# Spectral mixing in 32x32 blocks with shorter seams between the layers of a Fourier tower

## The chip, the cores and the metric

The kernel runs on one core of one Trainium2 chip. The metric is the device time of one execution in microseconds (us). Engines are named as in the profile: PE is TensorE (matmuls), PEld its weight loads, DVE is VectorE, ACT is ScalarE, POOL is GpSimd, SP is SyncE, which issues most DMAs.

## The reference, cut to what matters

A tower of four Fourier layers on 64 images of 64x64 pixels and 32 channels, a two-layer head to one value per pixel, then an attention and an expert stage (the second half, which the change leaves as it is):

```python
x = coords @ fc0_w + fc0_b                             # lift 3 -> 32 channels
for sw, cw, cb in layers:                              # 4 layers
    x_ft = rfft2(x, norm='ortho')
    out = einsum('bixy,ioxy->boxy', x_ft[:, :, :20, :20], sw)   # the mix
    x1 = irfft2(out padded to 64x33, norm='ortho')
    x2 = einsum('bchw,oc->bohw', x, cw) + cb
    x = gelu(x1 + x2)
x = gelu(x @ fc1_w + fc1_b) @ fc2_w + fc2_b
```

Only 20x20 frequencies of each image are kept. The mix multiplies, at each of these 400 frequencies, a 32x32 matrix of channels by the 32 channels of 64 images (real and imaginary part: 128 columns).

## The kernel before

All data is fp32, and each fp32 matmul is two weight loads and two matmul records in the trace (a high and a low part). The Fourier transforms are matmuls with constant tables, and between them DVE turns 32x32 blocks (STREAM_TRANSPOSE) so that the next axis comes to lie on the partitions.

The tower works on pairs of images (32 pairs, index t or j). Per layer it has two parts.

The mix (`mix`, line 478): it needs all images, so it stands between the layers. `modes` holds the frequencies: its partitions are four blocks of 32, block b = 2*kwh + khh, where kwh is the half of the row frequency kw (kw = 10*kwh + k) and khh the half of kh. For each k of 10 and each m of 10, two matmuls of 64x64 (kwh 0 and 1) with 128 columns run. Their weights are `mode_w`, two 32x32 matrices on the diagonal of a 64x64 block whose other half is zeros that the host wrote; they come by DMA in a ring of five k. The sums of one k fill four PSUM banks; two sets of four banks take turns. ACT copies the first half of a k (line 767), DVE the second (line 711) back into `modes` as 128x640, and the matmuls of k wait for the copies of k-2.

The pair loop: for each pair DVE turns the modes (`turn_modes`, line 679), PE does the inverse transform over h (`inverse_h`, line 491, banks 4 to 7), DVE turns the result (`turn_inverse`, line 689), PE adds the 1x1 convolution (`conv`, line 511: 16 matmuls of 32x32 on all 16 blocks of the array, banks 0 to 3) and the inverse transform over w (`inverse_w`, line 524, four parts, banks 0 to 3), ACT applies GELU (line 774) and stores the result. In the same loop, two and three pairs behind, the next layer's forward transform starts: DVE turns the activations (`turn_act`, line 654), PE does `dft_w` (line 429, banks 4 to 7), DVE `turn_w` (line 665), PE `dft_h` (line 441, banks 0 and 1), DVE `turn_h` (line 671), which writes `modes`. The loop of a layer has three extra rounds (j = 32 to 34) for the last forward transforms. `keep_busy` (line 517) are matmuls on constants whose result nobody reads; 8 stand behind the first `inverse_h` of a layer, 6 + 4 + 6 in the extra rounds, 10 ahead of the next mix.

The start: SP loads the identity (for the second half), the two forward tables, the first two quarters of the input, then it waits for the zeroed tiles (`zeroed`) and loads 14 small constants for the lift (`lift_consts`), then the later quarters and the rest. PE transforms four quarters of the input; 8 `lift` matmul groups (line 458, four 32x32 blocks each, ACT copies, line 759) follow each of them one quarter behind. DVE builds `lift_w` from the constants between `turn_w(0)` and `turn_w(1)` (line 698). Eight matmuls (line 545) that build the first layer's convolution weights stand ahead of the last lifts, and DVE copies them (line 705).

Every engine works through its list in the order written; waits are on semaphores.

Of the kernel before, what the change touches and what calls it, by code (L numbers as in the profile page):

```python
# [23 lines left out]
RING_W = 5  # L24
PAD_N = 96
MIXES = MODES // 2
GROUP = 16
# [19 lines left out]
def dft_constants():  # L47
# [39 lines left out]
    places = np.concatenate([np.arange(MODES // 2), 16 + np.arange(MODES // 2)])  # L87
# [120 lines left out]
def tower(nc, banks, front, h_dram, wqkv, k_rope, k_decay, x, x_turned, fc0, fc0_t, sw, cwt, cb, fc1_w, fc1_b, fc2_w, fc2_b,  # L208
# [4 lines left out]
    with ExitStack() as ctx:  # L213
# [24 lines left out]
        mode_w = sb("mode_w", [128, RING_W, MODES // 2, 2 * CH])  # L238
# [20 lines left out]
        fwd_in = sem("fwd_in")  # L259
# [6 lines left out]
        mode_w_in = [sem(f"mode_w_in{s}") for s in range(RING_W)]  # L266
# [13 lines left out]
        mixed = [sem(f"mixed{half}") for half in range(2)]  # L280
# [37 lines left out]
        def after_mix(l, k):  # L318
            return l * MIXES + k + 1
# [17 lines left out]
        def mix_sums(rows_b, k):  # L337

            return banks[rows_b, k % 2 * 4:k % 2 * 4 + 4, :].rearrange("p b n -> p (b n)")
# [11 lines left out]
        def _(sp):  # L351

            def load_mode_w(l, k):

                n = l * MIXES + k
                if n >= RING_W:
                    sp.wait_ge(mixed[1], n - RING_W + 1)
                sp.dma_start(flat(mode_w[:, n % RING_W]), sw[l, k]).then_inc(mode_w_in[n % RING_W], 16)
# [27 lines left out]
            for k in range(RING_W):  # L386
                load_mode_w(0, k)
            for q in range(2):
                sp.dma_start(flat(xin[:, q]), x[q]).then_inc(xin_in[q], 16)
            for l in range(LAYERS):  # L390
                for k in range(RING_W, MIXES):
                    load_mode_w(l, k)
                if l + 1 < LAYERS:
                    for k in range(RING_W):
                        load_mode_w(l + 1, k)
# [26 lines left out]
        def _(pe):  # L422

            def dft_w(n):

                for wh in range(2):
                    for i in range(2):
# [7 lines left out]
            def dft_h(n, parity):  # L435

                pe.wait_ge(w_turned, after_w_turned(n, 1))
                for ph in range(2):
                    for i in range(2):
                        for kwh in range(2):  # L440
                            mm = nc.tensor.matmul(banks[kwh * 64:(kwh + 1) * 64, i, 0:320],  # L441
# [7 lines left out]
            def lift(q, e):  # L449
# [4 lines left out]
                else:  # L454
                    pe.wait_ge(lift_w_set, 1)
                for b in range(4):
# [5 lines left out]
            def mix(l):  # L462
# [5 lines left out]
                for k in range(MIXES):  # L468
                    n = l * MIXES + k
                    pe.wait_ge(mode_w_in[n % RING_W], 16 * (n // RING_W + 1))  # L470
                    if k >= 2:
                        pe.wait_ge(mix_out["act"], after_mix(l, k - 2))
                        pe.wait_ge(mix_out["dve"], after_mix(l, k - 2))
                    for m in range(MODES // 2):
                        at = m // 5 * 2 * 512 + m % 5 * 128
                        for kwh in range(2):
                            rows_b = slice(kwh * 64, (kwh + 1) * 64)
                            mm = nc.tensor.matmul(mix_sums(rows_b, k)[:, at:at + 128],  # L478
                                                  mode_w[rows_b, n % RING_W, m, :],
                                                  modes[rows_b, :, k, 2 * m:2 * m + 2], start=True, stop=True)  # L480
                        if m % 5 == 4:
                            mm.then_inc(mixed[m // 5], 1)

            def inverse_h(l, t):

                pe.wait_ge(modes_turned, after_inverse(l, t))
                for i in range(2):
# [9 lines left out]
            def conv(l, t):  # L497

                if t > 0:
                    pe.wait_ge(inv_turned, after_inv_turned(l, t, 1))  # L500
                    pe.wait_ge(act_set, after_out(l, t - 1, 3))
                if l == 0:
# [11 lines left out]
            def keep_busy(n):  # L514

                for _ in range(n):
                    nc.tensor.matmul(banks[:, 3, 0:128], inv_w[:, 0, :], inv_w[:, 0, :], start=True, stop=True)
# [12 lines left out]
            pe.wait_ge(fwd_in, 32)  # L530
            pe.wait_ge(xturned_in[0], 16)
            dft_w(0)
            for q in range(QUARTERS):
# [7 lines left out]
                if q > 0:  # L541
                    for e in range(LIFT_E):
                        lift(q - 1, e)
            for e in range(LIFT_E):
                mm = nc.tensor.matmul(banks[:, 4, e * CH:(e + 1) * CH],
                                      fc0_cols[:, e].rearrange("c p e k -> c (p e k)"), conv_w[0:CH, 0, :],
                                      start=True, stop=True)
            mm.then_inc(first_w_filled, 1)
# [4 lines left out]
            pe.wait_ge(first_w_set, 1)  # L553

            for l in range(LAYERS):
# [3 lines left out]
                keep_busy(8)  # L559
                for j in range(PAIRS + (0 if last else 3)):  # L560
                    if j > PAIRS:
                        if j == PAIRS + 1:
                            pe.wait_ge(act_set, after_out(l, PAIRS - 1, 3))
                        keep_busy(6)
                    if j == 0:
                        conv(l, 0)
# [7 lines left out]
                    if j < PAIRS:  # L574
                        if j >= 4 and not last:
                            pe.wait_ge(modes_set, forward(l + 1, j - 4) + 1)
                        if j > 0:
                            conv(l, j)
                        for p in range(2):
                            inverse_w(l, j, p)  # L580
                    if 0 <= j - 2 < PAIRS and not last:
# [3 lines left out]
                        elif j >= PAIRS:  # L585
                            pe.wait_ge(w_turned, after_w_turned(forward(l + 1, j - 3), 1))
                        dft_w(forward(l + 1, j - 2))
                    if j < PAIRS:
                        for p in range(2, 4):
                            inverse_w(l, j, p)  # L590
                    if 0 <= j - 3 < PAIRS and not last:
                        if j < PAIRS:
                            pe.wait_ge(act_set, after_out(l, j, 1))
                        else:
# [1082 lines left out]
```

## Time and profile before

| what | value |
|---|---|
| runs | 1740.77, 1744.27, 1749.69 us (median 1744.27) |
| the profiled execution | 1742.08 us, its span 1740.3 us |
| PE / PEld / DVE / ACT / POOL busy | 94% / 55% / 69% / 34% / 8% |
| start up to the first mix | 0 to 53.9 us |
| the four mixes | 53.9 to 76.1, 390.8 to 412.9, 727.7 to 749.8, 1064.5 to 1086.7 us |
| between two mixes | 314.7 us each, three times |
| after the last mix | 653.6 us |

The span is the time from the first to the last instruction. The profiled execution lies 2.2 us under the median of the runs. A line of the trace's timeline has the start, the duration, engine, line and operation, output and inputs, the number of instructions merged, and in brackets the idle time before it and who ended it. A busy PE is one with a matmul in flight, and not one at its peak: a mix has PE busy all the time and uses two of four 64x64 blocks of the array.

### The profile page before, as it was taken

The page shows a single profiled execution, that of the slowest core. Times are in us where ns is not written, and L with a number is a line of the kernel's source. Part 1 is how long each engine was busy: PE and PEld are TensorE (multiplying, and loading weights), DVE is VectorE, ACT ScalarE, POOL GpSimd, SP SyncE. Part 2 cuts the span into 40 slices and gives each one's busy share as a digit, 9 for nine tenths or more (in the row PEclk, how much of TensorE's full clock was granted, in tenths as well). Part 3 has the DMA queues.
Part 4 walks back from the last instruction along what each step waited for, and adds up shares of the span by engine and source line. Part 5 has one row for each costly group of instructions (what it writes and reads, how often), then busy time and mean ns, then how long its engine had stood idle before and what let it go on. Part 6 is the DMA issues. An engine that isn't in the chain of part 4 may idle for free. (4 is left out here: it accounts for less than half of the span.)

```text
span 1740.3 us, 44221 instructions
## 1 busy us (share of the span) xinstructions
PE 1634.5 (94%) x20058; PEld 959.0 (55%) x20058; DVE 1201.5 (69%) x1406; ACT 585.3 (34%) x783; POOL 140.1 (8%) x64
## 2 busy tenths in 40 slices
PE   7999999999999999999999999999988888989996
PEld 2765555558555555775555557777741117833332
DVE  3389898875898898578898984555510007956777
ACT  2332232213232222232222322444468885510000
POOL 1000000000000000000000000000000000057664
PEclk9999999999999999999999999999999999999998
DMA  5233233244656556456556563699996642075551
GB/s 197 77 134 135 122 123 123 104 189 127 263 204 235 218 221 236 159 173 237 219 218 236 205 240 112 234 347 352 363 343 239 228 166 89 13 182 149 145 142 37
DMA packets 67706, 327.86 MB, mean 188 GB/s; under 512 B 19200, under 2 KB 21184, under 8 KB 33600
## 3 DMA queue, kind: packets, MB, share of 16 engines
q1 hardware_dynamic: 44736, 189.63, 33.3%
q10 hardware_dynamic: 22784, 135.41, 18.9%
q8 instruction: 159, 2.61, 0.6%
q14 instruction: 27, 0.22, 0.0%
HBM read 187.64 MB, written 137.36 MB: 187 GB/s over the span
## 5 line engine op out<-in xcount | busy, mean ns | idle before, releaser
L774 ACT ACTIVATE act_c<-slots,conv_b 128x512 f32<-128x512 f32 x512 | 352.3, 688 | 741.4 <-PE slots L524 741.4
L524 PEld LDWEIGHTS slots<-inv_w,inv_out 128*128 128x128 f32 x4096 | 499.1, 196 | 179.0 <-issue 179.0
L524 PE MATMUL slots<-inv_w,inv_out 128*128 128x128 f32 x4096 | 540.7, 287 | 0.0
L689 DVE STREAM_TRANSPOSE inv_out<-slots 128x1024 f32<-128x1024 f32 x256 | 304.5, 1228 | 101.0 <-PE slots L491 101.0
L665 DVE STREAM_TRANSPOSE turned_h<-slots 128x1024 f32<-128x1024 f32 x200 | 237.7, 1227 | 34.1 <-PE slots L429 33.8
L654 DVE STREAM_TRANSPOSE turned_w<-act_c 128x1024 f32<-128x1024 f32 x192 | 225.1, 1214 | 0.0
L429 PE MATMUL slots<-turned_w,fwd_w 32*64 32x512 f32 x3200 | 200.8, 609 | 13.0 <-DMA fwd_h<-in_k_fwd_h_dram 7.1
L1598 POOL TENSOR_TENSOR modes<-at_turned,modes 128x1024 f32<-128x1024 f32 x14 | 34.6, 2477 | 1545.7 <-DMA at_turned<-level_scratch 1530.6
L785 ACT ACTIVATE inv_out<-slots,b 128x1024 f32<-128x1024 f32 x128 | 135.7, 1111 | 20.8 <-PE slots L613 20.8
L671 DVE STREAM_TRANSPOSE modes<-slots 128x640 f32<-128x640 f32 x96 | 81.4, 848 | 88.2 <-PE slots L441 88.2
L441 PE MATMUL slots<-turned_h,fwd_h 64*64 64x320 f32 x1600 | 137.1, 455 | 0.0
L511 PE MATMUL slots<-act_c,conv_w 32*32 32x512 f32 x3072 | 110.7, 599 | 20.3 <-DVE modes L671 14.9
L491 PE MATMUL slots<-turned_k,inv_h 32*64 32x320 f32 x2048 | 101.9, 453 | 8.6 <-DVE turned_k L679 7.2
L429 PEld LDWEIGHTS slots<-turned_w,fwd_w 32*64 32x64 f32 x3200 | 60.2, 132 | 79.8 <-issue 61.8
L679 DVE STREAM_TRANSPOSE turned_k<-modes 128x640 f32<-128x640 f32 x128 | 102.9, 806 | 0.1
L1133 PE MATMUL slots<-modes,ex_lattice_w 128*64 128x512 f32 x344 | 89.3, 622 | 11.4 <-DVE modes L1340 5.8
L613 PE MATMUL slots<-act_c,w 32*64 32x512 f32 x1024 | 71.5, 612 | 21.7 <-ACT inv_out L785 20.9
L478 PE MATMUL slots<-modes,mode_w 64*64 64x128 f32 x1600 | 88.6, 267 | 0.8 <-ACT modes L759 0.8
L478 PEld LDWEIGHTS slots<-modes,mode_w 64*64 64x64 f32 x1600 | 87.7, 130 | 1.9 <-issue 1.5
L1340 DVE TENSOR_TENSOR modes<-slots,modes 128x512 f32<-128x512 f32 x102 | 65.2, 684 | 32.5 <-PE slots L1116 31.7
L746 DVE TENSOR_SCALAR modes<-slots,b 128x512 f32<-128x512 f32 x4 | 3.0, 751 | 113.9 <-PE slots L624 113.9
L711 DVE COPY modes<-slots 128x640 f32<-128x640 f32 x40 | 33.0, 824 | 69.7 <-PE slots L478 69.7
(145 smaller groups left out, 1057.4 us busy)
## 6 DMA issues: line engine op xcount, KB each, us to landing
act_scratch<-act_c ACTq DMA_DIRECT2D x128, 1024.0 KB, 4.9
act_c<-act_scratch SPq DMA_DIRECT2D x128, 1024.0 KB, 5.2
mode_w<-in_sw_dram SPq DMA_DIRECT2D x40, 320.0 KB, 3.0
at_turned<-level_scratch SPq DMA_DIRECT2D x36, 256.0 KB, 4.2
at_ret_t<-level_scratch SPq DMA_DIRECT2D x34, 256.0 KB, 4.1
turned_w<-in_x_turned_dram SPq DMA_DIRECT2D x4, 1024.0 KB, 5.7
xin<-in_x_dram SPq DMA_DIRECT2D x4, 1024.0 KB, 7.5
at_straight<-level_scratch SPq DMA_DIRECT2D x16, 256.0 KB, 4.1
```

The source lines that it names most:

```text
L429: mm = nc.tensor.matmul(banks[i * 64:(i + 1) * 64, 4 + p, :], fwd_w[p * 32:(p + 1) * 32, wh, :], turned_w[p * 32:(p + 1) * 32, n % 2, wh, ...
L441: mm = nc.tensor.matmul(banks[kwh * 64:(kwh + 1) * 64, i, 0:320], fwd_h[i * 64:(i + 1) * 64, parity, ph, :], turned_h[i * 64:(i + 1) * 64, ...
L478: mm = nc.tensor.matmul(mix_sums(rows_b, k)[:, at:at + 128], mode_w[rows_b, n % RING_W, m, :], modes[rows_b, :, k, 2 * m:2 * m + 2], start ...
L491: mm = nc.tensor.matmul(banks[half * 64:(half + 1) * 64, 4 + 2 * i + kwh, 0:320], inv_h[b * 32:(b + 1) * 32, l % 2, :], turned_k[b * 32:(b ...
L511: nc.tensor.matmul(banks[q * 32:(q + 1) * 32, p, :], w, src, start=True, stop=False, skip_group_check=True)
L524: mm = nc.tensor.matmul(banks[:, p, at:at + 128], inv_out[:, t % 2, i, p, :, :, r].rearrange("p b o -> p (b o)"), inv_w[:, i, :], start=Fa ...
L654: last = nc.vector.transpose(dst, src)
L665: nc.vector.transpose(dst, src).then_inc(w_turned, 1)
L679: nc.vector.transpose(dst, src).then_inc(modes_turned, 1)
L689: nc.vector.transpose(dst, src).then_inc(inv_turned, 1)
L774: nc.scalar.activation(act_c[:, t % RING, :, p, :], banks[:, p, :].rearrange("p (i m) -> p i m", i=2), ACT.Gelu, bias=conv_b[:, l:l + 1]). ...
L785: nc.scalar.activation(unit[:, n % 2, a:a + 2, :], banks[:, at:at + 2, :], ACT.Gelu, bias=b1[:, 0:1]).then_inc(unit_set, 1)
```

## The change

- The mix weights are stored as 32x32 matrices without the zeros (half the bytes); all ten k of a layer have their place in `mode_w`, loaded two k at a time.
- For an even k a block's result stays in its own partitions (b to b), for an odd k it goes to the other half's (b to b^2). An even and an odd k are mixed together (`side` 0 and 1), so 8 different 32x32 blocks of the array are named one after the other, then again for the next kh. The inverse table over w (`places`) undoes the exchange.
- A step u covers five kh of two k: 40 matmuls. After each, ACT copies side 0 and DVE side 1 (128x640 each), and step u waits for the copies of u-2.
- Behind the last step, both copy four images first (`few_set`), DVE turns the modes of pair 0, and then they copy the other 60 images. `keep_busy(8)` goes; `conv(0)` and the first part of `inverse_w(0)` come ahead of `inverse_h(1)`.
- The three extra rounds of a layer become a written-out tail: two of its `dft_h` use banks 2 and 3, so that they needn't wait for the `turn_h` of banks 0 and 1; `turn_act(31)` and `turn_w(30)` come ahead of `turn_h(28)`; 26 `keep_busy` matmuls become 6.
- `dft_h` waits for the two halves of `turn_w` one by one.
- Start: the first half of quarter 0 is loaded first, in a DMA of its own; the identity later; the lift constants are issued by ACT; 7 and 6 matmuls on zeros stand around the first `dft_w`; the eight matmuls for the first convolution weights come behind `dft_h(0)`, and ACT copies them.

```diff
-    places = np.concatenate([np.arange(MODES // 2), 16 + np.arange(MODES // 2)])
+    kw = np.arange(MODES)
+    place, kwh = kw % MIXES, kw // MIXES
+    places = 16 * (kwh ^ place % 2) + place
...
-            sp.dma_start(flat(fwd_w[:]), k_fwd_w).then_inc(fwd_in, 16)
-            sp.dma_start(flat(turned_w[:, 0]), x_turned[0]).then_inc(xturned_in[0], 16)
-            sp.dma_start(flat(fwd_h[:]), k_fwd_h).then_inc(fwd_in, 16)
+            sp.dma_start(flat(turned_w[:, 0, 0]), x_turned[0, :, 0:1024]).then_inc(first_half_in, 16)
+            sp.dma_start(flat(fwd_w[:]), k_fwd_w).then_inc(fwd_w_in, 16)
+            sp.dma_start(flat(turned_w[:, 0, 1]), x_turned[0, :, 1024:2048]).then_inc(xturned_in[0], 16)
             sp.dma_start(flat(turned_w[:, 1]), x_turned[1]).then_inc(xturned_in[1], 16)
-            sp.wait_ge(zeroed, 1)
-            for dst, src in lift_consts:
-                sp.dma_start(dst, src).then_inc(lift_in, 16)
+            sp.dma_start(flat(fwd_h[:]), k_fwd_h).then_inc(fwd_h_in, 16)
...
-                for k in range(MIXES):
-                    n = l * MIXES + k
-                    pe.wait_ge(mode_w_in[n % RING_W], 16 * (n // RING_W + 1))
-                    if k >= 2:
-                        pe.wait_ge(mix_out["act"], after_mix(l, k - 2))
-                        pe.wait_ge(mix_out["dve"], after_mix(l, k - 2))
-                    for m in range(MODES // 2):
-                        at = m // 5 * 2 * 512 + m % 5 * 128
-                        for kwh in range(2):
-                            rows_b = slice(kwh * 64, (kwh + 1) * 64)
-                            mm = nc.tensor.matmul(mix_sums(rows_b, k)[:, at:at + 128],
-                                                  mode_w[rows_b, n % RING_W, m, :],
-                                                  modes[rows_b, :, k, 2 * m:2 * m + 2], start=True, stop=True)
-                        if m % 5 == 4:
-                            mm.then_inc(mixed[m // 5], 1)
+                for u in range(MIX_STEPS):
+                    if u % 2 == 0:
+                        pe.wait_ge(mode_w_in[u // 2], 16 * (l + 1))
+                    if u >= 2:
+                        pe.wait_ge(mix_out["act"], after_mix(l, u - 2))
+                        pe.wait_ge(mix_out["dve"], after_mix(l, u - 2))
+                    for m in range(5):
+                        for side in range(2):
+                            for b in range(4):
+                                to = b ^ 2 * side
+                                rows_b, rows_to = slice(b * 32, (b + 1) * 32), slice(to * 32, (to + 1) * 32)
+                                k, kh = u // 2 * 2 + side, u % 2 * 5 + m
+                                mm = nc.tensor.matmul(mix_sums(rows_to, side, u % 2)[:, m * 128:(m + 1) * 128],
+                                                      mode_w[rows_b, u // 2, side, kh, :],
+                                                      modes[rows_b, :, k, 2 * kh:2 * kh + 2], start=True, stop=True)
+                    mm.then_inc(mixed, 1)
...
                 inverse_h(l, 0)
-                keep_busy(8)
+                conv(l, 0)
+                pe.wait_ge(inv_turned, after_inv_turned(l, 0, 1))
+                inverse_w(l, 0, 0)
+                inverse_h(l, 1)
+                for p in range(1, 4):
+                    inverse_w(l, 0, p)
...
                 if not last:
-                    keep_busy(10)
+                    parity = (l + 1) % 2
+                    ends = [forward(l + 1, PAIRS - 3 + i) for i in range(3)]
+                    pe.wait_ge(act_turned, after_turn(l + 1, PAIRS - 2))
+                    pe.wait_ge(w_turned, after_w_turned(ends[0], 1))
+                    dft_w(ends[1])
+                    pe.wait_ge(act_set, after_out(l, PAIRS - 1, 3))
+                    keep_busy(4, 3)
+                    dft_h(ends[0], parity, at=2)
+                    pe.wait_ge(act_turned, after_turn(l + 1, PAIRS - 1))
+                    pe.wait_ge(w_turned, after_w_turned(ends[1], 1))
+                    dft_w(ends[2])
+                    pe.wait_ge(modes_set, ends[0])
+                    dft_h(ends[1], parity)
+                    pe.wait_ge(modes_set, ends[0] + 1)
+                    dft_h(ends[2], parity, at=2)
+                    keep_busy(2, 4)
...
+                dve.wait_ge(mixed, after_mix(l, MIX_STEPS - 1))
+                nc.vector.tensor_copy(*mix_part(MIX_STEPS - 1, 1, slice(0, 4))).then_inc(few_set["dve"], 1)
+                dve.wait_ge(mix_out["dve"], after_mix(l, MIX_STEPS - 2))
+                dve.wait_ge(few_set["dve"], l + 1)
+                dve.wait_ge(few_set["act"], l + 1)
                 turn_modes(l, 0)
+                nc.vector.tensor_copy(*mix_part(MIX_STEPS - 1, 1, slice(4, IMAGES))).then_inc(mix_out["dve"], 1)
+                turn_inverse(l, 0)
                 turn_modes(l, 1)
-                turn_inverse(l, 0)
...
+                if not last:
+                    turn_act(l + 1, PAIRS - 1)
+                    turn_w(forward(l + 1, PAIRS - 2))
+                    for t in range(PAIRS - 4, PAIRS):
+                        if t == PAIRS - 2:
+                            turn_w(forward(l + 1, PAIRS - 1))
+                        turn_h(forward(l + 1, t), modes[:, 2 * t:2 * t + 2],
+                               at=2 if t in (PAIRS - 3, PAIRS - 1) else 0)
```

## Rows read from the trace of the kernel before

**Rows 1.** The page's head: the span of the profiled execution.

```profile
span 1740.3 us, 44221 instructions
```

**Rows 2.** Busy time by stretch: first mix, all up to the second.

```profile
53.93:76.10 22.17, 22.14 (x400) 21.94 (x400) 7.42 (x9) 7.29 (x11) 0.00 (x0) 1.00 0.45 134
76.10:390.80 314.70, 303.92 (x4166) 184.21 (x4165) 273.55 (x257) 89.08 (x129) 0.00 (x0) 1.00 0.34 130
```

**Rows 3.** Timeline of the second mix: PE, ACT's first copy, DVE's last copy.

```profile
390.80 22.15 PE L478 MATMUL slots<-modes,mode_w 64*64 64x128 f32 x400
...
392.16 0.69 ACT L767 COPY modes<-slots 128x640 f32<-128x640 f32 x1 [17.04 <-PE slots L478]
...
413.00 0.82 DVE L711 COPY modes<-slots 128x640 f32<-128x640 f32 x1 [1.37 <-PE slots L478]
```

**Rows 4.** DVE's copy line by itself: min, median and max in ns.

```profile
L711 DVE COPY modes<-slots x40: 823/825/825, 56.5 to 1086.7; 128x640 f32<-128x640 f32 x40
```

**Rows 5.** Timeline: matmuls on 32x32 blocks, a convolution and eight lifts.

```profile
22.95 6.00 PE L458 MATMUL slots<-act_c,lift_w 32*32 32x400 f32 x64
...
87.30 0.27 PEld L511 LDWEIGHTS slots<-xin,first_w 32*32 32x32 f32 x32 [0.63 <-issue]
87.33 1.15 PE L511 MATMUL slots<-xin,first_w 32*32 32x512 f32 x32
...
88.42 4.04 PE L524 MATMUL slots<-inv_w,inv_out 128*128 128x128 f32 x32
```

**Rows 6.** Timeline behind the second mix, PE and DVE.

```profile
413.85 1.57 DVE L679 STREAM_TRANSPOSE turned_k<-modes 128x640 f32<-128x640 f32 x2
414.75 0.80 PE L491 MATMUL slots<-turned_k,inv_h 32*64 32x320 f32 x16 [1.80 <-DVE turned_k L679]
...
415.66 2.38 DVE L689 STREAM_TRANSPOSE inv_out<-slots 128x1024 f32<-128x1024 f32 x2 [0.23 <-PE slots L491]
...
418.54 0.85 PE L491 MATMUL slots<-turned_k,inv_h 32*64 32x320 f32 x16
...
419.31 4.04 PE L524 MATMUL slots<-inv_w,inv_out 128*128 128x128 f32 x32
...
423.28 0.79 PE L491 MATMUL slots<-turned_k,inv_h 32*64 32x320 f32 x16
```

**Rows 7.** Timeline of a layer's last rounds, PE and DVE.

```profile
372.42 2.38 DVE L665 STREAM_TRANSPOSE turned_h<-slots 128x1024 f32<-128x1024 f32 x2 [3.04 <-PE slots L429]
...
374.32 1.36 PE L441 MATMUL slots<-turned_h,fwd_h 64*64 64x320 f32 x16
...
375.61 1.97 PE L429 MATMUL slots<-turned_w,fwd_w 32*64 32x512 f32 x32
...
376.52 2.33 DVE L654 STREAM_TRANSPOSE turned_w<-act_c 128x1024 f32<-128x1024 f32 x2
...
388.37 2.50 PE L517 MATMUL slots<-inv_w 128*128 128x128 f32 x20
388.51 0.85 DVE L671 STREAM_TRANSPOSE modes<-slots 128x640 f32<-128x640 f32 x1 [1.98 <-PE slots L441]
```

**Rows 8.** Timeline of the start: SP, PE and DVE.

```profile
6.49 4.23 SPq L380 DMA_DIRECT2D fc_cols<-in_fc_t_dram  x8
...
7.07 3.72 PE L429 MATMUL slots<-turned_w,fwd_w 32*64 32x512 f32 x32 [7.07 <-DMA fwd_h<-in_k_fwd_h_dram]
...
14.70 0.43 DVE L698 TENSOR_TENSOR lift_w<-fc_rows,lift_mask 128x256 f32<-128x256 f32 x1 [1.42 <-DMA fc_cols<-in_fc_t_dram]
...
19.76 1.98 PE L429 MATMUL slots<-turned_w,fwd_w 32*64 32x512 f32 x32 [0.73 <-DVE turned_h L665]
...
45.25 1.97 PE L545 MATMUL slots<-conv_w,fc_cols 32*128 32x32 f32 x16
...
47.25 0.42 DVE L705 COPY first_w<-slots 128x256 f32<-128x256 f32 x1 [6.96 <-PE slots L545]
```

**Rows 9.** A stretch without matmuls in the second half; the clock stands behind POOL.

```profile
1536.00:1540.00 4.00, 0.00 (x0) 0.00 (x0) 0.00 (x0) 0.00 (x0) 2.21 (x1) 0.67 0.99 237
```

More of the change, by code:

```diff
@@ L23 @@
 RING = 4
-RING_W = 5
 PAD_N = 96
 MIXES = MODES // 2
+MIX_STEPS = MIXES
 GROUP = 16
@@ L279, in tower @@
         lift_out = sem("lift_out")
-        mixed = [sem(f"mixed{half}") for half in range(2)]
+        mixed = sem("mixed")
         mix_out = {"dve": sem("mix_out_dve"), "act": sem("mix_out_act")}
@@ L334, in after_store, with mix_sums @@
             return 16 * (l * (PAIRS // RING) + t // RING + 1)
-        def mix_sums(rows_b, k):
-            return banks[rows_b, k % 2 * 4:k % 2 * 4 + 4, :].rearrange("p b n -> p (b n)")
+        def mix_sums(rows, side, half):
+            at = 4 - 4 * side + 2 * half
+            return banks[rows, at:at + 2, :].rearrange("p b n -> p (b n)")
         def head_bank(n, a):
@@ L385, in _ @@
                 sp.dma_start(dst, src).then_inc(rest_in, 16)
-            for k in range(RING_W):
-                load_mode_w(0, k)
+            sp.dma_start(ident[:, :], k_ident).then_inc(ident_in, 16)
+            for pair in range(MIXES // 2):
+                load_mode_w(0, pair)
             for q in range(2):
@@ L422, in _, with warm_up @@
         def _(pe):
+            def warm_up(n):
+                for _ in range(n):
+                    nc.tensor.matmul(banks[:, 3, 384:512], w2_at[:, 0:128], w2_at[:, 0:128], start=True, stop=True)
             def dft_w(n):
                 for wh in range(2):
+                    if n == 0 and wh == 1:
+                        pe.wait_ge(xturned_in[0], 16)
                     for i in range(2):
@@ L512, in conv, with keep_busy @@
                                          skip_group_check=True)
-            def keep_busy(n):
+            def keep_busy(n, b):
                 for _ in range(n):
-                    nc.tensor.matmul(banks[:, 3, 0:128], inv_w[:, 0, :], inv_w[:, 0, :], start=True, stop=True)
+                    nc.tensor.matmul(banks[:, b, 384:512], inv_w[:, 0, :], inv_w[:, 0, :], start=True, stop=True)
             def inverse_w(l, t, p):
@@ L540, in _ @@
                 dft_h(q, 0)
-                if q > 0:
+                if q == 0:
+                    pe.wait_ge(lift_in, LIFT)
+                    for e in range(LIFT_E):
+                        mm = nc.tensor.matmul(banks[:, 3, e * CH:(e + 1) * CH],
+                                              fc0_cols[:, e].rearrange("c p e k -> c (p e k)"), conv_w[0:CH, 0, :],
+                                              start=True, stop=True)
+                    mm.then_inc(first_w_filled, 1)
+                else:
                     for e in range(LIFT_E):
                         lift(q - 1, e)
[L544 to L548, printed above, removed]
             pe.wait_ge(modes_set, QUARTERS)
@@ L558, in _ @@
                 inverse_h(l, 0)
-                keep_busy(8)
[L560 to L566, printed above, removed]
+                conv(l, 0)
[4 more added lines that the diff above has]
+                    inverse_w(l, 0, p)
+                for j in range(1, PAIRS):
                     if j + 1 < PAIRS:
@@ L573, in _ @@
                         inverse_h(l, j + 1)
[L574 to L581, printed above, removed]
+                    if j >= 4 and not last:
+                        pe.wait_ge(modes_set, forward(l + 1, j - 4) + 1)
+                    conv(l, j)
+                    for p in range(2):
+                        inverse_w(l, j, p)
+                    if j >= 2 and not last:
                         pe.wait_ge(act_turned, after_turn(l + 1, j - 2))
@@ L584, in _ @@
                             pe.wait_ge(inv_turned, after_inv_turned(l, j + 1, 1))
-                        elif j >= PAIRS:
-                            pe.wait_ge(w_turned, after_w_turned(forward(l + 1, j - 3), 1))
                         dft_w(forward(l + 1, j - 2))
[L588 to L594, printed above, removed]
-                            pe.wait_ge(modes_set, forward(l + 1, j - 4) + 1)
-                        if j == PAIRS + 1:
-                            keep_busy(4)
+                    for p in range(2, 4):
+                        inverse_w(l, j, p)
+                    if j >= 3 and not last:
+                        pe.wait_ge(act_set, after_out(l, j, 1))
                         dft_h(forward(l + 1, j - 3), (l + 1) % 2)
                 if not last:
-                    keep_busy(10)
+                    parity = (l + 1) % 2
[14 more added lines that the diff above has]
+                    keep_busy(2, 4)
             pe.wait_ge(act_set, after_out(LAYERS - 1, PAIRS - 1, 3))
@@ L756, in _ @@
         def _(act):
+            act.wait_ge(zeroed, 1)
+            for dst, src in lift_consts:
+                act.dma_start(dst, src).then_inc(lift_in, 16)
+            act.wait_ge(first_w_filled, 1)
+            nc.scalar.copy(flat(first_w[:]), banks[:, 3, 0:LIFT_E * CH]).then_inc(first_w_set, 1)
             for n in range(PAIRS):
@@ L1635 @@
     sw = sw.transpose(0, 5, 4, 1, 6, 3, 2)
-    paired = _np.zeros(sw.shape[:6] + (2, CH), _np.float32)
-    for khh in range(2):
-        paired[:, :, khh, :, :, :, khh] = sw[:, :, khh]
     x = _np.concatenate([f["x"], _np.ones((IMAGES, HH, WW, 1), _np.float32)], axis=3)
```

100 lines of the change are left out of this document (55 added, 45 removed).

## The prediction

> **What bounds the kernel now.** I read the busy time by stretch first. Each of the four mixes is a stretch of 22.2 us in which PE runs the whole time while DVE and ACT are busy a third of it [rows 2]; the stretch between two mixes takes 314.7 us, 303.9 of them with matmuls in flight [rows 2]. PE sets the pace in both. The change leaves a pair's work alone, so I take the pair loop at nothing and look at three places: the mixes, the seams on either side of them, and the start. I read each in the timeline.
>
> **The mix.** 400 records take 22.15 us [rows 3], so 55.4 ns each. A record's 128 columns would pass at 2.4 GHz in 53 ns; a fp32 record takes two passes (107 ns), and two blocks run side by side. So the mix is bound by columns, with 110.8 ns per round of two blocks. After the change there are 800 records in rounds of eight blocks: 10 rounds per step (five kh, high and low part), 10 steps, 100 rounds. The trace of before has no round of eight blocks with 128 columns. The nearest is the convolution: 32 records of 32x32 on 16 blocks, with 512 columns, take 1.09 us up to the next line's start (87.33 to 88.42), and their 32 loads together cover 0.27 us, so each follows the last by some 5 ns [rows 5]. In a round of 110.8 ns eight starts fit at that spacing, so I take 110.8 ns for the new round too, and 1.11 us for a step.
>
> Then the copies. Before, ACT's first copy starts 1.36 us after the first of ten rounds [rows 3]; eight blocks instead of two stagger the end by some 0.05, so 1.41. DVE's copy takes 0.82 [rows 4], and I allow 0.05 back to PE: 2.28 us for the two steps that share the banks, 1.14 per step against PE's 1.11. Copies and matmuls nearly balance. The last copy can start after 4 x 2.28 + 1.11 + 1.41 = 11.64 us, where before it started after 22.20 (390.80 to 413.00) [rows 3]. That is 10.56 less. Weights: half the bytes, all resident a layer ahead; their wait is hidden as before, by the 300 us pair loop.
>
> At this place the Trainium skill speaks against the change. In "TensorE: Matmul & The Clock Gate", section "Wait — 56ns, not 53.3ns?", it says that matmuls never start closer than about 25 ns, however few columns they have. By that 800 records take 20 us, and a mix would give back 2 us instead of 10.6. The loads and blocks in [rows 5] start closer than that, so here the trace disagrees, though in bursts only.
>
> **Behind the mix.** Before: copy 0.82, turn of pair 0, and `inverse_h(0)` starts 1.75 us after the copy's start (413.00 to 414.75) [rows 3, 6]. Now a copy of four images (40 elements) stands in place of 640. From 0.82 for 640 [rows 4] and 0.42 for 256 [rows 8] it comes to 0.20, so 0.62 less. ACT's second copy (0.69 [rows 3]) ends under the turn. So far 11.18 per mix.
>
> From `inverse_h(0)` to `inverse_h(2)`, before, 8.53 us [rows 6], with 8 `keep_busy` among them. Now, counted from `inverse_h(0)`: DVE copies 60 images up to 0.75 (hidden, since the turn waits for the 0.91 of `inverse_h` anyway, as 414.75 to 415.66); `turn_inverse(0)` to 3.29, `turn_modes(1)` to 4.10; PE's convolution lies under it; `inverse_w(0,0)` 3.35 to 4.50 (8 records at 0.118 and a drain of 0.2); `inverse_h(1)`; DVE turns its result from 5.41 to 7.79, then the modes of pair 2 to 8.6: `inverse_h(2)` at 8.67. So DVE takes the place of `keep_busy` and 0.14 is lost. Per layer 11.04, four times: 44.2 us.
>
> **Ahead of the mix** (three times). Before, `dft_h(28)` starts at 374.32 and the mix at 390.80, 16.48 later; the last `turn_h` ends at 389.36, and 20 records of `keep_busy` hold PE another 1.4 us [rows 3, 7]. Now: DVE ends `turn_w(29)` at 374.80, does `turn_act(31)` to 377.5 (its input, ACT's last GELU, is in at 375.15), waits for `dft_w(30)` (375.61, done at 377.7), `turn_w(30)` to 380.05, `turn_h(28)`, `turn_h(29)` to 381.7. PE meanwhile: 8 records of `keep_busy`, `dft_h(29)` into the other banks, idle to 380.1, `dft_w(31)` to 382.1, `dft_h(30)`. DVE `turn_w(31)` 382.2 to 384.55, `turn_h(30)` to 385.4; `dft_h(31)`'s second half ends at 385.4, `turn_h(31)` at 386.3. Mix at 386.35: 4.45 less, 13.35 in all. Durations: 2.38, 2.33, 0.85, 1.90, 1.29 [rows 7]. The new tail is one chain of turns and transforms; what is late next is DVE.
>
> **The start.** Before, `dft_w(0)` takes 3.72 us at 7.07 and `dft_w(2)` 1.98 at 19.76 [rows 8]: the same work at half the speed, so PE's clock was at its lower level (1.2 GHz) at first. The matmuls on zeros and the earlier first half (half of the bytes, and the identity no longer ahead) bring `dft_w(0)` forward by some 3 us. But DVE must build `lift_w` before `turn_w(1)`, from 14 small DMAs. Now ACT issues them from about 2.5 (after the zeroing); at SP's pace (8 in 4.23 us [rows 8], 14 in 7.65) the last is out at 10.15, and it landed 3.98 after its issue (10.72 to 14.70 [rows 8]): 14.1, or 13.1 with a shorter landing. I take 13.7. Then `turn_w(1)` ends at 16.5, and `dft_w(2)` starts at 16.65: 3.1 less (2.0 to 4.7). The 1.9 us of matmuls for the first weights [rows 8] go into PE's wait for that turn. Together 5.0.
>
> **Sum.** 44.2 + 13.35 + 5.0 = 62.5; 1742.08 - 62.5 = 1679.6 on the profiled execution, whose span is 1740.3 [rows 1]. It ran 2.2 us below the median. I say 1680.
>
> **Rivals.**
> 1. Slower: dispatch, not columns, paces a long run. 55.4 ns per record [rows 3] would then be the price of a record of any size, and 800 take 44.3 us: 22.15 more per mix, 88.6 in all, less the other gains (62.5 - 42.2 = 20.3): 1810. It decides from 27.2 us per mix, that is 34 ns per record. Against it: the convolution's 32 records average 34 with four times the columns, and 64 lifts in 6.0 us wait for ACT half of the time [rows 5]. But both are short bursts behind a wait, and a mix is 1600 PE instructions without pause. 0.05.
> 2. A floor on starts of up to 34 ns, the convolution's average [rows 5]: 27.2 us per mix, 1742, no change. 0.05. With the page's 25 ns it would be 20 us per mix and 1713.
> 3. Blocks that share 32 rows take turns, since even and odd k stream different data through the same rows: a mix stays at 22.15, only the rest is gained: 1722. The convolution streams four through the same rows in 2 x 512 columns' time [rows 5]; against that its data lies dense and the mix's in 8-byte pieces. 0.07.
> 4. Copies set the pace: they balance with PE within 3%, so a quarter more on the step (1.14 to 1.43) costs 2.9 per mix: 1691. 0.08.
> 5. The clock falls in a seam, since `keep_busy` goes. The trace shows the granted clock at a mean of 0.67 in a stretch without any matmul, 1536 to 1540 [rows 9], and PE had 1.80 us idle ahead of `inverse_h(0)` at full clock [rows 6]. The new gaps are 1.2 to 1.5 us, two close together. Half speed for 7 us costs 3.5 per seam, 14 in all: 1694. 0.10.
> 6. More than forecast, from a start that is not held by the constants or a seam without drains: 1673 to 1668. 0.07.
>
> **How the numbers follow.** The forecast has 0.58. The range goes from 1668 to 1706: it holds the forecast and cases 4 to 6 and leaves out 1 to 3 (0.17). A measurement of this kernel can tell about 0.5% (9 us) from no change. Slower is case 1; same is most of case 2; all else is faster: 0.91, 0.04, 0.05.
>
> **What would show it.** Line 478's successor: 800 records of 32x32 in about 11.5 us per mix, DVE's copies following each other at 1.14 us; at 22 it is case 3, at 44 case 1, and copies without gaps mean case 4. A granted clock of 1.00 between the mixes rules out case 5. From one mix's start to the next, 336.9 us before, I expect 321.4. `dft_w` of the third quarter near 16.7 us. The prediction is wrong if a mix takes over 13 us, or if the pair loop, which I took at nothing, moves.

## The result and the profile after

The change makes the kernel faster, by less than half of what was forecast: 1725.38 us in the median of four runs (1721.60 to 1725.98) against 1744.53 before (four runs), a ratio of 0.987 with an interval of 0.984 to 0.991. The prediction said 1680, with 1668 to 1706 as its range. The profiled execution took 1721.60 us, its span 1719.6. Medians below are of all executions of a kernel; ratios and intervals leave out the few that were disturbed, such as two of the twelve of e7_old_start, whose median without them is 1739.9.

The spans differ by 20.7 us. The table goes stage by stage; each number, in us, is the difference of two starts in the timelines of the two kernels.

| stage | before | after | forecast |
|---|---|---|---|
| start up to the first mix | 53.9 | 50.8 | 48.9 |
| mix's first matmul to `inverse_h(0)`, four mixes | 23.95 each | 21.5, 24.2, 22.1, 21.3 | 12.8 each |
| `inverse_h(0)` to `inverse_h(2)` | 8.53 each | 8.7, 9.3, 9.3, 9.2 | 8.67 each |
| `dft_h(28)` to the mix, three times | 16.48 each | 12.17, 12.17, 12.18 | 12.03 each |

So 3.1 came from the start, 6.8 from the mixes, 12.9 from the seams ahead of them, and the seams behind them cost 2.4: 20.4 in all. The pair loop, taken at nothing, took its old time. What is missing against the forecast is almost all in the mixes: 44.7 us were expected from that row, 6.8 came.

The first mix after, PE alone, in the timeline (start, duration, engine, line, operation, number of records, idle time before and its cause); before, a mix was one line of 22.15 us without a gap (the second mix, [rows 3]):

```profile
50.84 3.81 PE L491 MATMUL slots<-modes,mode_w 32*32 32x128 f32 x239 [0.66 <-issue]
...
55.53 2.18 PE L491 MATMUL slots<-modes,mode_w 32*32 32x128 f32 x127 [0.88 <-issue]
...
59.02 2.26 PE L491 MATMUL slots<-modes,mode_w 32*32 32x128 f32 x127 [1.30 <-issue]
...
62.44 2.04 PE L491 MATMUL slots<-modes,mode_w 32*32 32x128 f32 x128 [1.16 <-issue]
...
66.00 2.29 PE L491 MATMUL slots<-modes,mode_w 32*32 32x128 f32 x127 [1.52 <-issue]
...
69.97 1.06 PE L491 MATMUL slots<-modes,mode_w 32*32 32x128 f32 x52 [1.68 <-issue]
```

Two things are to be seen. Inside a burst (records without a pause between them) the blocks of the array work nearly as forecast: 239 records in 3.81 us are 16 ns each, eight array blocks side by side. And every 127 or 128 records PE stands still for 0.9 to 1.7 us, for no engine and no DMA ("issue"). 128 records and their 128 weight loads are 256 instructions. The page of the kernel after shows the same number in its list of DMA queues:

```profile
q8 instruction: 170, 2.79, 0.7%
```

170 packets carry 2.79 MB, 16.4 KB each, while PE has 43,000 matmul and load instructions in all: 253 per packet, some 64 bytes for an instruction. The Trainium skill, "Vector Engine (DVE) Microarchitecture Reference", section "2.1 Why there are multiple struct shapes", gives 64 bytes as the width of every instruction; the trace agrees for PE. PE's program comes from memory by DMA, a block of 256 instructions at a time, and in the mix the blocks come more slowly than eight array blocks use them up. By stretch, the first and the last mix after. The columns are the stretch, its length, the busy time (number) of PE, PEld, DVE, ACT and POOL, the granted clock, the busy share of the DMA engines and GB/s:

```profile
50.84:71.10 20.26, 13.65 (x800) 11.40 (x800) 7.44 (x10) 6.26 (x10) 0.00 (x0) 1.00 0.23 69
...
1045.72:1065.70 19.98, 13.60 (x800) 11.49 (x800) 7.42 (x9) 6.25 (x9) 0.00 (x0) 1.00 0.02 4
```

PE is busy 13.6 us of 20; its four hundred matmuls are twice as many as before. The last mix has nearly no DMA traffic beside it (4 GB/s) and takes as long as the first with 69, so it isn't the other transfers that set the pace of the instructions. That they cost them nothing is not shown: in the second mix, with 112 GB/s, the bursts start 3.8 to 3.9 us apart, in the last 3.4 to 3.7.

### The profile page after: what moved, and what is told of

Read it like the earlier page. It is cut to its first block and busy times, and to the rows that moved or that the text cites. A ratio compares the mean times of both kernels' runs of the same rounds, so it can differ in the third digit from the quotient of the medians.

```text
span 1719.6 us, 47103 instructions
## 1 busy us (share of the span) xinstructions
PE 1587.7 (92%) x21500; PEld 900.3 (52%) x21500; DVE 1201.3 (70%) x1409; ACT 585.9 (34%) x788; POOL 140.4 (8%) x64
## 3 DMA queue, kind: packets, MB, share of 16 engines
q8 instruction: 170, 2.79, 0.7%
## 5 line engine op out<-in xcount | busy, mean ns | idle before, releaser
L439 PEld LDWEIGHTS slots<-turned_w,fwd_w 32*64 32x64 f32 x3200 | 59.6, 131 | 69.4 <-issue 54.4
L638 PE MATMUL slots<-act_c,w 32*64 32x512 f32 x1024 | 71.5, 612 | 22.1 <-ACT inv_out L831 20.5
L491 PE MATMUL slots<-modes,mode_w 32*32 32x128 f32 x3200 | 54.5, 268 | 31.1 <-issue 30.1
L451 PEld LDWEIGHTS slots<-turned_h,fwd_h 64*64 64x64 f32 x1600 | 51.2, 131 | 46.2 <-issue 5.4
```

The costliest lines, as they stand in the source:

```text
L451: mm = nc.tensor.matmul(banks[kwh * 64:(kwh + 1) * 64, at + i, 0:320], fwd_h[i * 64:(i + 1) * 64, parity, ph, :], turned_h[i * 64:(i + 1) ...
```

## The experiments

Theory A: the supply of instructions, one block of 256 in no less than about 3.5 us. Its rivals: B, array blocks that share rows collide; a price per start; C, the copies set the pace.

**e1_sides64.** Four 64x64 blocks in place of eight of 32x32. The exchange between the halves stays, the zeros come back, and 800 instructions do for 1600. The weights come in ten portions of 320 KB per layer, five of them resident.

```diff
-                            for b in range(4):
-                                to = b ^ 2 * side
-                                rows_b, rows_to = slice(b * 32, (b + 1) * 32), slice(to * 32, (to + 1) * 32)
+                            for b in range(2):
+                                to = b ^ side
+                                rows_b, rows_to = slice(b * 64, (b + 1) * 64), slice(to * 64, (to + 1) * 64)
```

> The changed kernel with the mix weights again as 64x64 blocks with zeros (as before), but with even and odd k mixed together and exchanged between the halves as in the change: four 64x64 blocks at once, 200 matmuls (800 PE instructions) per mix in place of 400 (1600). Theory A, instruction supply: in the changed kernel's mixes PE works in bursts of 127 or 128 records with pauses of 1.3 to 1.9 us, and a 16 KB instruction packet arrives every 3.4 to 3.9 us; 800 instructions need no more than three of them, so the mix takes what the array needs, 100 rounds of 0.11 us: 11.3 to 13 us, without pauses, and the time falls from 1725 by about 35 to 1690 us. Theory B, the streams: different data streamed through the same rows collide; this kernel does that too, so its mix stays at 20 to 22 us and the time at 1722 to 1730. Theory C, the copies set the pace: steps stay as long as they are, 1725.

Measured: 1690.46 us, 0.967 of the kernel before (0.964 to 0.970). The first two mixes, PE:

```profile
53.12 12.34 PE L494 MATMUL slots<-modes,mode_w 64*64 64x128 f32 x400 [0.66 <-issue]
...
375.39 7.78 PE L494 MATMUL slots<-modes,mode_w 64*64 64x128 f32 x256 [0.33 <-DVE modes L700]
384.46 4.37 PE L494 MATMUL slots<-modes,mode_w 64*64 64x128 f32 x144 [1.29 <-issue]
```

A mix takes 12.2 to 13.4 us from its first record to the end of its last. The first and the fourth have no pause, the second has a single one, behind record 256, and the third one of 0.54 us: a little more than A had allowed (11.3 to 13 us, no pauses). The time fell as A said. B and C are out for this kernel, whose streams share rows and whose copies are the same. 64 of these matmuls are one block of instructions and take 3.9 us (half of the 7.78), so the array runs at the edge of the supply. In a second set of executions the same kernel took 1694.03 (e6_sides64_again, 0.970, 0.967 to 0.973).

> The same kernel as e1_sides64, for comparison on one chip: 0.966 to 0.967 of the kernel before; first mix between 50.8 and 53.1 us, by the landing of the constants.

**e3_diagonal64.** The same without the exchange (`to = b`, and the old `places`).

> As the first kernel of this set (64x64 blocks, 800 PE instructions per mix), but without the exchange between the halves: only the two blocks on the diagonal work, with the changed kernel's seams and start. Theory A: bound by columns like the kernel before, 200 rounds of 0.11 us, 22.2 us per mix without pauses; about 1 us more per layer than the changed kernel, 1726 to 1732 us. Against e1 it gives the worth of the exchange alone (about 40 us by A, none by B).

```profile
53.50 22.15 PE L494 MATMUL slots<-modes,mode_w 64*64 64x128 f32 x400 [0.66 <-issue]
```

Measured: 1729.63 us, 0.990 of before (0.984 to 0.995); every mix 22.15 us without a pause. The exchange, which lets all four 64x64 blocks work, is worth 39 us on the same chip (1729.63 to 1690.46). The run also gives the worth of all that isn't the mix's matmuls: 20.7 us in the medians (1750.28 to 1729.63), but with an interval of 8 to 28. Its profile shows 14.7 up to the start of the fourth mix. What follows `inverse_h(0)` of the last layer, most of it the second half, which none of the changes touches, takes from 651.8 (before) to 659.0 us (here) in the profiles without a probe.

**e2_half_columns.** The changed kernel with 64 columns per matmul, so that it leaves half of the mix out; eight matmuls at the start write zeros into all banks. One execution.

```diff
-                                mm = nc.tensor.matmul(mix_sums(rows_to, side, u % 2)[:, m * 128:(m + 1) * 128],
+                                mm = nc.tensor.matmul(mix_sums(rows_to, side, u % 2)[:, m * 128:m * 128 + 64],
...
-                                                      modes[rows_b, :, k, 2 * kh:2 * kh + 2], start=True, stop=True)
+                                                      modes[rows_b, 0:IMAGES // 2, k, 2 * kh:2 * kh + 2], start=True, stop=True)
```

> The changed kernel with each mix matmul on 32 of 64 images (64 columns in place of 128), the same number of instructions and copies. It leaves half of the mix out, and eight matmuls at the very start write zeros into all banks (a few us there). Theory A: the array has half the work and nothing changes, mixes stay at 20 to 22 us from first to last record, in shorter bursts with longer pauses. Theory B: the mix falls to 10 to 12 us. Theory C: unchanged in length, but the copies would follow each other without gaps.

Measured: 1727.96 us. Half the columns, and the mixes take 18.9 to 22.2 us from first to last start, as in the changed kernel. Part of the second mix:

```profile
388.12 1.53 PE L491 MATMUL slots<-modes,mode_w 32*32 32x64 f32 x127 [1.31 <-issue]
391.69 2.33 PE L491 MATMUL slots<-modes,mode_w 32*32 32x64 f32 x127 [2.04 <-issue]
395.59 2.32 PE L491 MATMUL slots<-modes,mode_w 32*32 32x64 f32 x127 [1.56 <-issue]
399.53 2.10 PE L491 MATMUL slots<-modes,mode_w 32*32 32x64 f32 x128 [1.62 <-issue]
```

The first of these bursts is shorter, as A said; the later ones are not. The granted clock is 1.00 up to 389.5 us and at its lower level (0.50, 1.2 GHz) from 391.5 us on:

```profile
392.00:400.00 8.00, 4.81 (x288) 4.07 (x279) 3.30 (x4) 2.77 (x4) 0.00 (x0) 0.50 0.31 86
```

So half the columns mostly pass at half the speed, and the array's time per record is nearly that of the changed kernel. This run by itself therefore can't tell B from A by its length. What speaks for A in it are the pauses, 1.3 to 2.0 us for nothing that the profile shows, behind every 127 or 128 records. That columns don't set the pace is shown by the next run, with 4 of them.

**e4_probe.** The disputed cost by itself: 512 matmuls of 4 columns, twice.

```diff
+            def probe(n, bank):
+
+                for i in range(n):
+                    b, q = i % 4, i // 4 % 4
+                    rows_b = slice(b * 32, (b + 1) * 32)
+                    mm = nc.tensor.matmul(banks[q * 32:(q + 1) * 32, bank + b, 384:388],
+                                     inv_w[rows_b, 0, 0:32], inv_w[rows_b, 0, 0:4], start=True, stop=True)
...
```

> The changed kernel plus twice 512 fp32 matmuls of 32x32 with 4 columns (1024 records, 2048 instructions each time, all 16 blocks in turn), once ahead of the second mix and once at the end of the tower, where few DMAs run. Theory A: both take 23 to 30 us, in bursts of 127 or 128 records with a new 16 KB packet every 3.4 to 3.9 us. If instead each start has a price of its own (25 ns), the records are evenly spaced over 26 us with no pauses. If only the array counted, under 10 us.

Measured: 1784.34 us in one execution. Some bursts of the first probe and of the second, PE, then the rate of all DMAs during the first one, in 40 slices of 384 to 413 us, and the queue of the instructions on the page:

```profile
398.72 1.35 PE L541 MATMUL slots<-inv_w 32*32 32x4 f32 x128 [2.38 <-issue]
402.18 1.35 PE L541 MATMUL slots<-inv_w 32*32 32x4 f32 x128 [2.11 <-issue]
405.63 1.34 PE L541 MATMUL slots<-inv_w 32*32 32x4 f32 x128 [2.11 <-issue]
...
1466.31 1.36 PE L541 MATMUL slots<-inv_w 32*32 32x4 f32 x128 [2.66 <-issue]
1470.05 1.35 PE L541 MATMUL slots<-inv_w 32*32 32x4 f32 x128 [2.38 <-issue]
```

```profile
GB/s 441 215 316 362 384 237 68 11 0 0 0 23 0 0 0 0 23 0 0 0 0 23 0 0 0 0 23 0 0 0 0 23 0 0 0 0 23 0 0 0
...
q8 instruction: 186, 3.05, 0.7%
```

The probes take 29.4 and 27.5 us. 128 records of almost no work run in 1.35 us (10.5 ns each, so no price of 25 ns per start), then PE waits; the next burst starts 3.45 to 4.0 us after the last. The 4096 instructions that the probes add to PE's came in 16 packets more than the changed kernel's 170: 256 in each. The row of DMA rates shows the blocks themselves: when nothing else moves, one short pulse (23 GB/s over 0.73 us, 16.4 KB) every fifth slice, that is every 3.6 us. This is A, with the cost measured: at 3.45 us for 256 PE instructions it is 27 ns per record with its load. With 4 columns as with 64 or 128, the bursts start as far apart, so B is out for the 32x32 blocks too. In the mixes of all runs on 32x32 blocks full bursts start 3.3 to 4.3 us apart, 3.7 to 3.9 in the mean of a run.

**e7_old_start and e9_old_start_13.** The start was to be tested by undoing it (e7), with the changed kernel beside it (e8_after_again, 1730.58 us, 0.990, 0.987 to 0.994).

```diff
-            pe.wait_ge(warm_zeroed, 1)
-            warm_up(7)
...
-            warm_up(6)
...
+            sp.wait_ge(zeroed, 1)
+            for dst, src in lift_consts:
+                sp.dma_start(dst, src).then_inc(lift_in, 16)
```

> The changed kernel with the start of the kernel before (order of the first DMAs, constants issued by SP, no matmuls on zeros, first convolution weights ahead of the last lifts). First mix at 53.9 us again. The prediction gave the start 5.0 us; the profiled execution of the changed kernel shows 3.1, and the profiles of e1, e2 and e3 only 0.4 to 1.3. By the prediction the time rises 5 us over the changed kernel's on the same chip, by the constants' theory 0.5 to 3.

> The changed kernel itself, for comparison on one chip: 0.987 of the kernel before. First mix between 50.8 and 53 us; pauses in the mixes as in the first profile.

Measured: 1740.14 us (0.996, 0.994 to 0.998), 9.6 more than the changed kernel, more than any of the theories allowed. But in the profiles the first mix begins at 54.2 us with the old start and at 54.4 in e8: the start itself gave nothing there. The loss lies in the mixes: 25.8, 27.4, 25.1 and 25.0 us up to `inverse_h(0)`, where e8 has 22.3, 23.2, 22.4 and 21.4. That is 14.0 us in sum; 3.7 of them come back in the seams behind the first three mixes, where the clock was at its lower level for longer in e8's profile. The first burst tells why the mixes are longer. It is 138 records with the old start and 239 in the changed kernel:

```profile
54.21 2.20 PE L492 MATMUL slots<-modes,mode_w 32*32 32x128 f32 x138 [0.81 <-ACT modes L796]
57.95 2.30 PE L492 MATMUL slots<-modes,mode_w 32*32 32x128 f32 x127 [1.54 <-issue]
```

The old start has 13 matmuls fewer, 26 records, so every mix begins 26 records earlier in the stream of instructions. What is left of the running block would be 111 + 26 = 137 records, more than a block holds: 9 are left of the block before, with one at hand behind it. So the mix has 137 records at hand in place of 239, and one more block has to be waited for. To test this, 13 matmuls that nobody needs were added to the old start:

```diff
+            for _ in range(13):
+                nc.tensor.matmul(banks[0:32, 4, 384:388], inv_w[0:32, 0, 0:32], inv_w[0:32, 0, 0:4], start=True, stop=True)
```

> e7_old_start plus 13 fp32 matmuls of 32x32 with 4 columns ahead of the first mix, whose results nobody reads. They bring the number of PE instructions ahead of the first mix back to that of the changed kernel (13 matmuls, 52 instructions, which the old start lacks). Block theory: instructions come in blocks of 256 (128 records), and what counts is where in a block a mix begins. In the changed kernel the first burst of the four mixes is 239, 115, 245 and 248 records, that is 111 to 120 left in the running block and mostly one more block at hand; 26 records more make it 9 to 18 plus 128, and e7_old_start's bursts are 138, 141 and 147: one more block must be waited for in each mix, and its mixes take 23.5 to 25.9 us in place of 19.7 to 22.7. With the 13 matmuls the first bursts go back to about 240 and the mixes to 20 to 22.7 us; though work is added, the time falls by 6 to 12 us against e7_old_start. If e7's longer mixes come from anything else, nothing changes, or it gets 0.3 us slower.

> e7_old_start again, for comparison on one chip: 0.996 of the kernel before; first bursts of the mixes near 138, 141, 143 and 147 records; mixes 23.5 to 26 us.

Measured on one chip: 1738.72 us without them, 1731.51 with them. Work was added and 7.2 us went. The third mix with them:

```profile
720.55 3.91 PE L492 MATMUL slots<-modes,mode_w 32*32 32x128 f32 x245 [0.33 <-DVE modes L696]
725.74 2.09 PE L492 MATMUL slots<-modes,mode_w 32*32 32x128 f32 x128 [1.28 <-issue]
```

The first bursts are 112, 115, 245 and 248 records, where the changed kernel has 239, 115, 245 and 248 (the second block of the first mix came 0.24 us late). The intervals against the kernel before (0.988 to 0.995 and 0.993 to 0.998) overlap a little; the mixes in the two profiles, 22.8, 23.9, 22.6 and 22.3 against 24.6, 27.3, 24.8 and 24.7 us up to `inverse_h(0)`, don't.

**e5_late_lift.** e1_sides64 with nothing ahead of the first lift that needs the small constants.

```diff
             turn_w(0)
-            dve.wait_ge(lift_in, LIFT)
-            nc.vector.tensor_tensor(lift_w[:], across(fc0_rows[:, :], LIFT_E), along(mask[:, :], CH),
-                                    ALU.mult).then_inc(lift_w_set, 1)
             for q in range(QUARTERS):
                 if q + 1 < QUARTERS:
                     turn_w(q + 1)
                 turn_h(q, in_modes[:, 2 * q:2 * q + 2])
+                if q == 0:
+                    dve.wait_ge(lift_in, LIFT)
+                    nc.vector.tensor_tensor(lift_w[:], across(fc0_rows[:, :], LIFT_E), along(mask[:, :], CH),
+                                            ALU.mult).then_inc(lift_w_set, 1)
```

> e1_sides64 with one more edit at the start: DVE builds the lift weights behind the turns of quarter 1 and of quarter 0's frequencies, and PE computes the first convolution weights behind the third quarter's dft_w, so that nothing before the first lift waits for the 14 small constants. In the profiles so far DVE waited 1.4 to 5.1 us for them, and where it waited longest PE sat idle and its next transforms ran at half speed (3.3 to 3.7 us in place of 1.98). If the constants' landing is what ate the start's gain: dft_w of the third quarter starts near 16 us in place of 18.6 to 19.9, at full speed, and the first mix near 50.3 us; 1 to 3 us less than e1_sides64. If something else holds the start, no change.

The start of e1_sides64, then that of e5_late_lift:

```profile
16.36 0.43 DVE L727 TENSOR_TENSOR lift_w<-fc_rows,lift_mask 128x256 f32<-128x256 f32 x1 [5.07 <-DMA fc_cols<-in_fc_t_dram]
...
19.23 3.62 PE L442 MATMUL slots<-turned_w,fwd_w 32*64 32x512 f32 x32 [0.88 <-DVE turned_h L694]
```

```profile
16.32 1.98 PE L442 MATMUL slots<-turned_w,fwd_w 32*64 32x512 f32 x32 [1.33 <-DVE turned_h L694]
```

In e1, DVE stood 5.07 us for the constants, PE ran dry with it, and its next transform took 3.62 us, half speed. In e5 it starts 2.9 us earlier at full speed, and the first mix begins at 50.5 us, where e1 and e6 have 53.1 and 52.9. The place was right. In the medians it is 1692.51 against 1694.03 us for e6, which these runs can't tell from no change.

## Why the prediction was wrong

**The mix** is the step that failed: "In a round of 110.8 ns eight starts fit at that spacing, so I take 110.8 ns for the new round too". The spacing was read from bursts behind a wait, where the instructions lay ready, and taken for a long run. It was also read too small: the row's 0.27 us for 32 loads are 8.4 ns each, and the probe has 10.5 ns per record; but eight of these, 84 ns, still fit into the round. The round itself was 11 to 15% too short at 110.8 ns: e1's rounds of four 64x64 blocks take 123 ns (12.34 us by 100), and the 239 records of the first burst after are 30 rounds in 3.81 us, 127 ns each. What was missing is a term of its own: 1600 instructions are 6.25 blocks, at 3.7 us each 23 us, less the one or two blocks at hand, whatever the array does. The mixes measured 20.0 to 22.9 us up to the end of their last record, where the forecast had some 11.5. Before, 800 instructions in 22 us stayed under that rate, so no row of before shows a pause by it, but the sum could have set 1600 instructions in 11.6 us against the 800 in 22.2: almost four times the rate of the mix before, and no long stretch in the rows is denser. Rival 1 names the danger ("a mix is 1600 PE instructions without pause"), and then prices it per record at all or nothing.

**Rival 2** gave, with the page's 25 ns, 20 us per mix and 1713 us; the mixes do take 20 to 23 us. The mechanism is another, though. The Trainium skill's floor of 25 ns between starts ("TensorE: Matmul & The Clock Gate", section "Wait — 56ns, not 53.3ns?") does not hold here, for matmuls that go to different blocks of the array: the probe's records start 10.5 ns apart inside a burst. The mean over a long run, 27 ns in the probe, is that of the supply. That the two come out alike is chance.

**The copies** were never the bound: DVE's idle time ahead of them is 57.0 us in sum, on the page of after. Rival 4 is out. So is rival 3: e1's four 64x64 blocks, two on the same rows, take 123 ns per round of four, where two took 110.8 before.

**Behind the mix** the four-image copy did its part: in e3, where nothing starves, the mix's first matmul to `inverse_h(0)` is 23.42 us (before 23.95, forecast 0.62 less), and on to `inverse_h(2)` 8.74 (forecast 8.67). In the changed kernel it is 9.2 to 9.3 in three layers. That is rival 5, a small part of it. The stretches behind the second mix after (the clock stands behind POOL):

```profile
402.00:406.00 4.00, 1.78 (x65) 1.01 (x65) 1.71 (x3) 0.76 (x2) 0.00 (x0) 0.87 0.26 81
406.00:410.00 4.00, 3.44 (x49) 1.24 (x40) 3.11 (x3) 0.00 (x0) 0.00 (x0) 0.70 0.03 12
```

The granted clock falls to its lower level (1.2 GHz) for part of each, behind a mix in which PE had paused two fifths of the time (13.6 us busy of 23.0); `inverse_h` and `conv` there take 1.37 and 2.05 us in place of 0.80 and 1.19. The seams have lost `keep_busy` in every run, so its lack alone doesn't lower the clock: on 64x64 blocks, with few pauses or none in the mix, one seam of 16 was longer than 8.74 us (e1, e3, e5, e6), and that one, 9.30 in e6, stands behind a mix with pauses. On 32x32 blocks 19 of 28 were, at 9.2 to 11.3 us (the changed kernel and e2, e4, e7 to e10). The pauses make the fall likely, but they don't decide it: the first mix after paused a third of its time and e9's last three as much as the changed kernel's, and behind these the clock stayed at 1.00. What decides it is open.

**Ahead of the mix** the reckoning along the chain held: 12.17 us for 12.03 forecast, 12.9 of 13.35 in the sum.

**The start** was put at 5.0 and gave 3.1 in the profile of after, 0.4 to 1.3 in those of e1, e2, e3, e4 and e6, and nothing in e8, where the first mix begins at 54.4 us. Its terms were mis-sized. The second half of quarter 0 landed 7.2 us after its issue, so that the first `dft_w` ended no earlier than before in that run. In the same run the eight matmuls for the first weights, which were to fit into a wait, end only at 18.6 us, 0.6 behind the turn that `dft_w` of the third quarter waits for. And the 13.7 us for the constants came out as 14.8 to 17.1; the sum had them as the bound, but not that PE, idle meanwhile, would lose its clock. In e8 against e7 nothing at all of the start's gain is left.

**The sum.** With half the instructions in the mix and all else as planned (e1) the kernel takes 1690 us, ten more than the 1680 that were forecast for 32x32 blocks: the rest of the sum was off mainly by a mix of 12.2 to 13.4 us in place of some 11.5 and by the start.

## What to carry to other kernels

Count the instructions of an unrolled stretch, not only its columns: here PE's program arrives at 256 instructions per 3.7 us or so (3.3 to 4.3), so a long stretch that needs more than some 70 per us waits for it, however well the array is filled. When tiling a matmul more finely, prefer the coarsest blocks that fill the array: here zeros in the weights cost less than instructions (64x64 with zeros beat 32x32 without by 37 us on the same chip, 1694.03 against 1730.58). And read a rate from a stretch as long as the one that is planned.

## What the runs showed of the hardware that was not expected

- PE's instructions come in blocks of 16.4 KB, 256 instructions, and behind a full burst the next starts 3.3 to 4.3 us after it did (3.45 to 4.0 in the probe, with no other traffic too). What sets this time (a packet itself is in transfer for about 1.1 us: 0.7% of 16 engines over 1719.6 us, by 170 packets), and whether other engines have the same limit, wasn't tried.
- About one block is at hand beyond the running one: first bursts of a mix are what is left of the running block plus 128 records, 239 to 248 in three mixes of the changed kernel. In its second, 115, the next block came 0.67 us late; why it was late is open. So the place of a code stretch in its block matters: 13 useless matmuls made the kernel 7.2 us faster.
- While instructions are at hand, matmuls on 16 array blocks of 32x32 start 10.5 ns apart with 4 columns.
- Pauses of 1 to 2 us within a stretch that is otherwise full can be followed by a lower granted clock behind it (19 of 28 seams, against 1 of 16 where the mix has few pauses or none), and in e2_half_columns, with less work per burst, inside it. Which stretches it hits was not explained by any run.
